# Macaron transformer block on one core: row maxima split into fp16 parts on GpSimd, one fp16 transpose and one copy per half, placed one head group later

## The reference

```
x = x + 0.5 * ffn(layernorm(x))       # x: 16 sequences of 256 tokens, 256 wide
x = x + attn(layernorm(x))
x = x + 0.5 * ffn(layernorm(x))
ffn:  hidden = silu(x @ wu.T) * (x @ wg.T);  hidden @ wd.T      # 1024 hidden, ternary weights w
attn: 16 query heads of 16, 4 key/value groups; scores / 4, causal mask, softmax, times v
```

## Time and profile before

| what | value |
|---|---|
| median of 3 runs | 611.13 us |
| span of the profiled execution | 610.4 us; no other time of it is listed, and it lies 0.7 under the median |
| TensorE busy | 566.9 us (93% of the span) |
| VectorE, ScalarE, GpSimd busy | 485.1, 411.1, 184.6 us |
| chain that ended last | TensorE 79%, VectorE 12%, ScalarE 6%, issue 2%, DMA 1% |

### The profile page before, as it was taken

The page is one execution under the profiler, slowest core; times in us unless marked ns, Lnnn a source line. Parts: engine busy times, 40 slices in busy tenths (PEclk is TensorE's granted clock), DMA queues, the critical chain, the costliest instruction groups (busy, mean ns, idle before and its releaser), DMA issues.

```text
span 610.4 us, 12447 instructions
## 1 busy us (share of the span) xinstructions
PE 566.9 (93%) x4276; PEld 346.0 (57%) x4276; DVE 485.1 (79%) x1854; ACT 411.1 (67%) x776; POOL 184.6 (30%) x231
## 2 busy tenths in 40 slices
PE   2869999999989989999899989998899999999998
PEld 2336566555656855656565656554445655666665
DVE  6998978989866889888988987888298687856654
ACT  4637765765635368898889888887866656665741
POOL 3115101110510234555545454557731011101100
PEclk9999999999989999999999999999999999999999
DMA  8601001100205161414141424230111111211112
GB/s 317 207 18 36 18 19 35 35 19 18 36 8 119 24 134 55 91 54 91 55 90 56 91 62 88 84 58 4 36 35 34 53 53 36 69 50 56 35 35 70
DMA packets 71679, 37.90 MB, mean 62 GB/s; under 512 B 33984, under 2 KB 71104, under 8 KB 71616
## 3 DMA queue, kind: packets, MB, share of 16 engines
q1 hardware_dynamic: 71616, 37.11, 23.9%
HBM read 18.22 MB, written 10.49 MB: 47 GB/s over the span
## 4 chain that ended last, share of the span: by engine, by line
PE 79%; DVE 12%; ACT 6%; issue 2%; DMA 1%; DVEq 0%
PE bank L1107 32%; PE bank L1119 17%; PE bank L1206 7%; PE bank L1270 6%; PE bank L1261 5%; PE bank L1233 5%; PE bank L1284 2%; PE bank L1275 2%; DVE hl L847 2%; ACT shared L587 2%; DVE sm_out L969 2%; DVE hid L832 2%; DVE stats L711 1%; PE bank L1098 1%; PE bank L1244 1%
## 5 line engine op out<-in xcount | busy, mean ns | idle before, releaser
L969 DVE CUSTOM_DVE_ANT_0 sm_out<-bank,mask 128x256 f16<-128x256 f32 (+1 forms) x512 | 153.0, 352 | 28.3 <-PE bank L1233 26.4
L477 ACT ACTIVATE silu<-bank,w_scale 128x512 f32<-128x512 f32 x128 | 87.3, 682 | 117.5 <-PE bank L1107 117.5
L832 DVE SCALAR_TENSOR_TENSOR hid<-silu,h_unit,bank 128x512 f32<-128x512 f32 x128 | 95.0, 742 | 63.4 <-ACT silu L477 63.2
L587 ACT ACTIVATE shared<-bank,qk_scale 128x512 f32<-128x512 f32 x192 | 121.2, 675 | 22.7 <-PE bank L1261 22.0
L1119 PE MATMUL bank<-wT_down,hh 128*128 128x256 f16 x512 | 118.7, 273 | 5.5 <-DVE hl L847 5.3
L1119 PE MATMUL bank<-wT_down,hl 128*128 128x256 f16 x512 | 118.7, 273 | 0.0
L847 DVE TENSOR_TENSOR hl<-hid,hh 128x512 f16<-128x512 f32 x128 | 102.9, 804 | 0.0
L1107 PE MATMUL bank<-xh,wT_gate 128*128 128x512 f16 x256 | 97.1, 379 | 4.8 <-DVE hid L832 4.8
L409 POOL TENSOR_TENSOR xnl<-xn,xnh 128x1024 f16<-128x1024 f32 x14 | 30.1, 2150 | 233.9 <-ACT xn L514 199.0
L1107 PE MATMUL bank<-xh,wT_up 128*128 128x512 f16 x256 | 98.0, 383 | 1.2 <-DVE xl L776 1.2
L1107 PE MATMUL bank<-xl,wT_up 128*128 128x512 f16 x256 | 97.9, 383 | 0.0
(11 more groups left out here) (113 smaller groups left out, 751.3 us busy)
## 6 DMA issues: line engine op xcount, KB each, us to landing
q_st<-q_scratch SPq DMA_DIRECT2D x32, 256.0 KB
q_scratch<-q_hl SPq DMA_DIRECT2D x16, 256.0 KB, 2.2
out_dram<-x SPq DMA_DIRECT2D x7, 512.0 KB, 2.9
x<-in_x_dram SPq DMA_DIRECT2D x1, 3072.0 KB, 15.8
k_scratch<-k_hl SPq DMA_DIRECT2D x16, 128.0 KB, 2.4
k_st<-k_scratch SPq DMA_DIRECT2D x16, 128.0 KB
x<-in_x_dram SPq DMA_DIRECT2D x2, 512.0 KB, 4.4
shared<-in_w_up_t_dram SPq DMA_DIRECT2D x2, 512.0 KB, 6.1
```

The source lines that it names most:

```text
L477: act.activation(silu[:, e % 2, :], U[e % 2][:, :], ACT.Silu, scale=w_scale[:, 0:1]).then_inc(silu_ready, 1)
L587: act.activation(prob[:, place % 2, i, :], ST[(3 * place + i) % 2][:, :], ACT.Exp, scale=qk_scale[:, 4:5]).then_inc(exp_done, 1)
L832: dve.scalar_tensor_tensor(out=hid[:, e % 4, :], in0=silu[:, e % 2, :], scalar=h_unit[:, 0:1], in1=GT[e % 2][:, :], op0=ALU.mult, op1=ALU. ...
L969: ins = dve.tensor_tensor_reduce(sm_out[:, i, cols], SM[i][:, cols], mask[:, S - size:S], 1.0, MASKED, ALU.add, ALU.max, rowmax[:, seq_par ...
```

## The change

The row maxima take another way, and one iteration later. VectorE's `row_max` now writes minus the maximum over 4096 at once (a minimum in place of the maximum). GpSimd splits it (`max_parts`, L357 a cast to fp16 and L359 a subtraction, each over 128x16) in g = 0 and 2. In g = 1 and 3 TensorE transposes both parts together in fp16 (one instruction, 32 rows), ScalarE copies them once (L565, 32x128 fp16), and `load_max` waits for that copy. Every piece of the two transfers is now 256 bytes for one head and one tile of queries. `q_st` is laid out sequence by sequence.

Beside that: GpSimd normalises a chunk in four steps of 128x256, each a subtraction and a multiplication with scalars per row (L393), in `normed_chunk` and at the end of the attention in `normed_parts`, whose high part becomes a copy; the third attention chunk is normalised by ScalarE at the stage's start; and `NORM_PLACES` becomes (0, 1), (0, 3), (1, 1), (1, 3), pairs of (odd sequence, g).

```diff
-                sp.wait_ge(mxlo_ready, 2 * b + half + 1)
+                sp.wait_ge(mx_ready, 2 * b + half + 1)
...
                     for g in range(G):
-                        if g in (0, 2) and not (last and k == 3):
+                        if g in (1, 3) and not (last and k == 3):
                             load_max(b + 1, k + 1, g // 2)
...
-            def max_rest(b, half):
-                pool.wait_ge(mx_ready, 2 * b + half + 1)
-                if not isinstance(b, int) or b > 0:
-                    pool.wait_ge(mx_loaded[half], 32 * b)
-                pool.tensor_tensor(mx_hl[:, half, 1, :], mx_32[:, half, :], mx_hl[:, half, 0, :],
+            def max_parts(b, half):
+                pool.wait_ge(sm_done, 3 * (G * b + 2 * half + 2))
+                if b:
+                    pool.wait_ge(mxT_ready, 2 * b + half - 1)
+                heads = rowmax[:, b % 2, :, half * HH:(half + 1) * HH].rearrange("p t h -> p h t")
+                pool.tensor_copy(mx_q[:, half, 0, :, :], heads).then_inc(mxhi_ready, 1)
+                pool.wait_ge(mxhi_ready, 2 * b + half + 1)
+                pool.tensor_tensor(mx_q[:, half, 1, :, :], heads, mx_q[:, half, 0, :, :],
                                    ALU.subtract).then_inc(mxlo_ready, 1)
...
+                for t in range(TT):
+                    ins = pool.tensor_scalar(xn[:, t, :], x[:, TT * (q % NC) + t, :], mv[:, n, at + t, 0:1],
+                                             rstd[:, n, at + t:at + t + 1], ALU.subtract, ALU.mult)
...
-                act.activation(mx_hl[:, half, 0, :], maxima[0:HH, :], ACT.Copy, scale=-1.0 / MAX_UNIT)
-                act.activation(mx_32[:, half, :], maxima[0:HH, :], ACT.Copy,
-                               scale=-1.0 / MAX_UNIT).then_inc(mx_ready, 1)
+                act.activation(mx_hl[:, half, :], maxima, ACT.Copy).then_inc(mx_ready, 1)
...
-            NORM_PLACES = [(0, 3), (1, 0), (1, 2), (1, 3)]
+            NORM_PLACES = [(0, 1), (0, 3), (1, 1), (1, 3)]
...
-            def max_transposes(b, k, half):
-                pe.wait_ge(sm_done, 3 * (G * b + 2 * half + 2))
+            def max_transposes(b, half):
+                pe.wait_ge(mxlo_ready, 2 * b + half + 1)
...
-                        if g in (0, 2) and not end:
-                            max_transposes(b + 1, k + 1, g // 2)
+                        if g in (1, 3) and not end:
+                            max_transposes(b + 1, g // 2)
```

More of the change, by code:

```diff
@@ L114, in macaron_block @@
         vT = sb("vT", [G * DH, TC])
-        q_st = sb("q_st", [P, 2, H, TC], F16)
+        q_st = sb("q_st", [P, 2, 2, H, S], F16)
         k_st = sb("k_st", [P, 2, G, TC], F16)
@@ L121, in macaron_block @@
         sm_out = sb("sm_out", [P, 3, 2 * S], F16)
-        mx_hl = sb("mx_hl", [HH, 2, 2, S], F16)
-        mx_32 = sb("mx_32", [HH, 2, S])
+        ident16 = sb("ident16", [P, P], F16)
+        mx_q = sb("mx_q", [P, 2, 2, HH, QT], F16)
+        mx_hl = sb("mx_hl", [2 * QT * HH, 2, P], F16)
         o_rec = sb("o_rec", [P, 2, H])
@@ L329, in _ @@
                                     base=0, pattern=[[-1, P]], channel_multiplier=1))
+            step(pool.tensor_copy(ident16[:, :], ident32[:, :]))
             pool.memset(ones[:, :], 1.0).then_inc(const_ready, 1)
@@ L388, in centre_chunk @@
                 pool.wait_ge(last_read, count)
[L389 to L402, removed]
+                for t in range(TT):
+                    ins = pool.tensor_scalar(xn[:, t, :], x[:, TT * (q % NC) + t, :], mv[:, n, at + t, 0:1],
+                                             rstd[:, n, at + t:at + t + 1], ALU.subtract, ALU.mult)
+                ins.then_inc(xn_ready, 1)
             def low_part(n, q):
@@ L576, in max_copy @@
                     act.wait_ge(mx_loaded[half], 32 * b)
-                maxima = FIRST_MT if isinstance(b, int) and b + half == 0 else MT
-                act.activation(mx_hl[:, half, 0, :], maxima[0:HH, :], ACT.Copy, scale=-1.0 / MAX_UNIT)
-                act.activation(mx_32[:, half, :], maxima[0:HH, :], ACT.Copy,
-                               scale=-1.0 / MAX_UNIT).then_inc(mx_ready, 1)
+                maxima = FIRST_MT if b + half == 0 else MT
+                act.activation(mx_hl[:, half, :], maxima, ACT.Copy).then_inc(mx_ready, 1)
             def exps(n, place, parts):
@@ L643, in attention @@
                 act.activation(silu[:, 0, 0:1], silu[:, 0, 0:1], ACT.Exp)
+                for t in range(TT):
+                    normed_tile(NC + 2, 6, t)
                 key_high(1)
@@ L1237, in max_scores @@
                     ins.then_inc(sm_ready, 1)
-            def max_transposes(b, k, half):
-                pe.wait_ge(sm_done, 3 * (G * b + 2 * half + 2))
-                if not (isinstance(b, int) and b == 0 and half == 0):
+            def max_transposes(b, half):
+                pe.wait_ge(mxlo_ready, 2 * b + half + 1)
+                if b + half:
                     pe.wait_ge(mx_ready, 2 * b + half)
-                for qt in range(QT):
-                    ins = pe.transpose((FIRST_MT if isinstance(b, int) and b + half == 0 else MT)[0:HH, qt * P:(qt + 1) * P], rowmax[:, k % 2, qt, half * HH:(half + 1) * HH],
-                                       ident32[:, :])
-                ins.then_inc(mxT_ready, 1)
+                pe.transpose(MT if b + half else FIRST_MT, mx_q[:, half, :, :, :].rearrange("p a h t -> p (a h t)"),
+                             ident16[:, :]).then_inc(mxT_ready, 1)
             def scores(n, b, k, g, parts=range(3)):
@@ L1358, in attention @@
                 pe.wait_ge(res_done, NT + 2)
[L1359 removed]
+                max_transposes(0, 1)
                 val_transposes(1, (qkv_lo, 5))
```

64 lines of the change are left out of this document (28 added, 36 removed).

## The result

The changed kernel is slower: 631.98 us median of 4 runs (629.31 to 636.97) against 611.12 (611.08 to 612.34), a ratio of 1.034 with a 95% interval of 1.030 to 1.038. I had forecast 601.9. The profiled execution has a span of 629.1, that of before 610.4: 18.7 to explain.

A forecast was written before the change was run, and what follows sets the result against it. The prediction took TensorE to bound the kernel, apart from waits for ScalarE and VectorE. Gains of 4.2 + 1.5 + 1.6 + 0.9 + 1.0 = 9.2 took 611.1 to 601.9 us, range 594.5 to 609.5.

The forecast's parts named there:

- what is late next: Steady attention: half 1 of the maxima, behind eight reads, lands at 310.5; its reader waits 1.1 to 1.4, or 2.0.
- 1.6 for the six cycles: Steady attention: gain kept despite late half 1, about 0.45 a Newton cycle and 0.1 another.
- The clock: Rival: TensorE's pauses in even 1 lower the clock, 1.8 each; 607.3 for three, 614 for all; chances 0.10 and 0.10.
- First feed-forward, 4.2: First feed-forward: short GpSimd pieces let VectorE step in between, shrinking TensorE's gap and keeping the clock; gain 4.2 us.
- the head's 0.9: First sequence and a half of attention, ahead of the first wait: 0.55 of transposes and 0.3 of copies gained.
- the rival at 0.17: GpSimd's pieces take 0.63 and up; the two feed-forward gains fall from 5.7 to about 1.3: 606.3; chance 0.17.
- Second feed-forward, 1.5: Where the attention ends: two of GpSimd's three passes become four short pieces, the third a copy; gain 1.5 us.
- Steady attention, 1.55 a cycle taken alone: Attention cycle: transposes 0.66, ScalarE waits 0.45 and 0.89 saved, less 0.45; 1.55 a cycle, 9.3 over six.
- Last pair, 1.0: Last two sequences: fewer copies and transposes, no 0.72 wait for row maxima, transfers perhaps 0.7 late; gain 1.0 us.
- In time: Rival: half 1 arrives in time, the six waits vanish, cycles gain 9.3 in place of 1.6: 594.2; chance 0.13.

The follow-up runs named there:

- run 4: Kernel before the change, with SyncE issuing the two transfers of half 1 of the maxima behind the eight reads in odd 2: 625.13 us, ratio 1.021.
- run 5: Changed kernel with the odd sequence's four reads moved to odd 3, behind half 1's transfers, the other four staying in odd 2: 605.58 us, ratio 0.990.
- run 6: Changed kernel with 40 matmuls of no use to the output filling TensorE's waits for half 1: 624.88 us, ratio to before 1.021.
- run 8: Changed kernel with half 1's two transfers that follow reads issued by ScalarE on its own queue: 611.02 us, ratio to before 0.999.
- run 10: Run 9's kernel with `NORM_PLACES` as before the change: 607.91 us, ratio to before 0.993.
- run 7: Kernel before the change with only GpSimd's two passes over a chunk made four subtract-and-multiply pieces, third chunk left on GpSimd: 608.11 us, ratio 0.994.
- run 9: Run 5's kernel with GpSimd's two operations on half 0 of the last sequence put ahead of that iteration's mask: 603.08 us, ratio to before 0.986.
- run 1: Changed kernel with SyncE's eight reads moved to odd 3, behind half 1's two transfers: 605.88 us, ratio to before 0.990.

## Why the prediction was wrong

- **The step that failed** is in the part on what is late next: "So half 1 lands about 2.5 after 308.0". What stood ahead of it held in the first cycle: I had the reads start 6.8 ahead of the reader, and they start 7.1 ahead of it (240.31, and the pause that begins at 247.4); I had 5.43 for their issue, and it takes 5.32. But half 1 lands 4.66 after it. I had followed the engines only until their share first fell, at 2.1 (0.35), where in the changed kernel they are busy until 2.9, with a trickle of bytes for 0.75 behind it. And I took the data's move for the landing, though the landing comes 1.0 later. That is 2.2 too little a time, six times; the waits are 2.5 to 4.3 where I had 1.1 to 2.0. Run 4 shows that it was wrong for the old layout already, by 1.3 to 2.0. The term of the sum that hung on it, 1.6 for the six cycles, came out at -21.8 with the clock.
- **What I left out:** a write of q that lands late. I took the median of 2.2 for every cycle; 4.0 to 4.7 stand in the traces of runs 4, 5, 6, 8 and 10. The changed kernel's six waits don't rest on it (2.2 in the first cycle, 2.36 in the second), but a schedule with less than 2 us of slack there does.
- **The clock** was the rival on the slower side, at 0.20, with 614 for all six falls. With waits of 2.5 to 4.3 the pauses lie about the 2.96 that had lost the clock before, and four of six lost it; a fall costs 1.65 (I had 1.8), and filling the pauses gives 7 (run 6). Whether the clock falls hung on the same wrong landing.
- **First feed-forward, 4.2 and the head's 0.9:** 4.55 came, and run 7 gives 4.3 for the feed-forward's part alone. The size held, but by luck: the reason was wrong. I had short pieces between which VectorE steps in; they are 1.21 to 1.52 long, and VectorE is hardly held by them (hl 0.75 beside one; two of its small steps 0.33 and 0.34, others 0.17). By my own formula such pieces would have given nearly nothing, the rival at 0.17.
- **Second feed-forward, 1.5:** nothing came; it is 0.2 longer. The wait of 1.2 for hl is still there. Beside the pieces hl is fast, but GpSimd's chunk takes as long as before (4.83 + 1.42 + 2.13 us against 1.90 + 1.89 + 1.89 + 2.40), and its low part now holds one hl for 2.62.
- **Steady attention, 1.55 a cycle taken alone:** run 9 gives 1.23 in a cycle (28.98 - 27.75), 0.44 in a Newton cycle. In a Newton cycle a wait for VectorE of 1.18 takes the place of ScalarE's: VectorE's busy time in such a cycle goes from 26.23 to 27.34, as the masks now start with two of the Newton steps (0.56 and 0.55 long in place of 0.16). I had not asked what the earlier exponential would bring GpSimd to do.
- **Last pair, 1.0:** -1.2 came, from the wait of 1.67 for GpSimd and a fall of the clock behind it (0.93), where I counted only the maxima of VectorE. Without that wait, in run 9, 1.0 comes (21.49 against 22.45).
- **"In time", 594.2:** run 9 is that case, 603. Of its 9.7 us between the spans, 4.4 come ahead of the first cut, 4.6 in the five cycles, nothing in the next stretch, 1.0 in the last pair and -0.2 behind it. My rival lacked the 1.18, that next stretch and the second feed-forward.

## What to carry to other kernels

A transfer of 4 KB behind 1.3 MB of reads does not land when the reads have been issued: here it landed 4.2 to 4.8 us after that. Take the time from the last issue to the landing from a trace as one number, and ask of every delayed load what its queue will hold by then. Give a transfer on which others wait some slack beyond its median: the write of q took up to 4.7 us against 2.4. Where the forecast pause of TensorE comes near one behind which a trace already shows the clock fall, add the fall to the price. And on GpSimd and VectorE the form of the instruction can decide more than its length: a longer one that holds VectorE hardly at all was worth 4 us.

## What the runs showed of the hardware

- GpSimd's tensor_scalar with two scalars per partition takes 1.21 us for 128x256, 1.52 at one place, and VectorE's two-input hl beside it 0.75. GpSimd's tensor_tensor of 1.90 us made hl 2.40, the low part of 2.13 made it 2.62. The Trainium skill ("SBUF — State Buffer", section "Who interferes with whom") has a VectorE instruction with two SBUF inputs contend with any GpSimd instruction that reads SBUF. The trace agrees for GpSimd's two-input forms and the mask, and in the other direction for GpSimd's 128x16 subtraction beside VectorE's xnl (1.27 in place of 0.22); for tensor_scalar it hardly does, and the measurement decides. The 128x16 cast also takes 0.65 in place of 0.20 beside VectorE's cast, which has one input.
- Granted clock: TensorE pauses of 2.92, 3.65, 3.35 and 4.31 us, and 3.75 in run 4, stand in cycles with a lower clock; 2.71, 2.49 and, in run 4, 2.01 and 1.97 in cycles at 1.00; but one of 2.00 in run 10 in a cycle at 0.95, and behind the 1.67 of the last pair it falls in the changed kernel and in runs 1, 5 and 8 (0.93) and not in run 6. The length of a pause alone does not tell.
- A transfer of 4 KB lands 1.7 us after its issue (median), 2.5 to 3.0 behind four reads (runs 5, 9 and 10), 3.6 to 4.1 behind eight in the changed kernel and 2.9 to 3.7 in run 4, and once 3.42 with nothing ahead of it. Another engine's queue does not shorten this: 3.5 to 4.7 in run 8.
- A write of q of 256 KB lands 2.4 us after its issue (median; 2.2 in the old order), and single ones 4.0 to 4.7.
